# The queries of two heads issued in pairs on TensorE, in slots three, five, six and seven of each group

## What is computed

```python
x = x + tanh(g_xattn) * xattn(ctx_1024, layernorm(x))   # 8 heads of 128
x = x + tanh(g_ffn) * moe(layernorm(x))                 # 8 experts, the best 2 of each row
# xattn(media, latents), per batch element:
q = ln(latents) @ Wq + bq
k, v = split(concat(ln(media), ln(latents)) @ Wkv + bkv)
out = softmax(q @ k.T / sqrt(128)) @ v @ Wo + bo
```

## Time and profile before

| | |
|---|---|
| median of 3 runs | 797.5 us |
| lowest and highest run | 796.06 and 798.2 us |
| the profiled execution, span from first to last instruction | 795.7 us |
| TensorE busy | 760.7 us, 96% of the span, 5392 matmuls |
| TensorE weight loads | 643.6 us, 81% |
| VectorE busy | 528.3 us, 66% |
| ScalarE busy | 496.9 us, 62% |
| GpSimd busy | 446.1 us, 56% |
| mean granted TensorE clock | 0.993 of full speed |

### The profile page before, as it was taken

How to read it: one execution, slowest core, us unless ns; L and a number is a source line. 1 busy time by engine, 2 the same in 40 slices (tenths; PEclk the granted TensorE clock), 3 DMA queues, 4 the chain that set the end, 5 groups by cost and what they waited for, 6 DMA issues and landing times.

```text
span 795.7 us, 17460 instructions
## 1 busy us (share of the span) xinstructions
PE 760.7 (96%) x5392; PEld 643.6 (81%) x5392; DVE 528.3 (66%) x1829; ACT 496.9 (62%) x1630; POOL 446.1 (56%) x455
## 2 busy tenths in 40 slices
PE   7999999999999999999999999999999999979788
PEld 6778777777888988778988878898877888868765
DVE  5636677685857567677658776776868567565536
ACT  3677777676766566766656667565567665554522
POOL 2233264646552544785655586665568566556664
PEclk9999999999999999999999999999999999999999
DMA  7735151542454642174754226664414555634523
GB/s 198 209 150 194 60 213 69 211 146 81 145 188 154 205 153 72 38 231 143 237 189 143 65 76 218 206 212 163 127 54 140 180 191 188 212 112 116 154 77 87
DMA packets 119791, 119.42 MB, mean 150 GB/s; under 512 B 14585, under 2 KB 94994, under 8 KB 119698
## 3 DMA queue, kind: packets, MB, share of 16 engines
q1 hardware_dynamic: 111088, 102.41, 39.1%
q0 software_dynamic: 7680, 15.74, 6.8%
q10 hardware_dynamic: 930, 0.15, 0.1%
HBM read 35.94 MB, written 41.55 MB: 97 GB/s over the span
## 4 chain that ended last, share of the span: by engine, by line
PE 77%; issue 6%; POOL 6%; DVE 5%; ACT 4%; DMA 1%; another core or an unknown queue 1%; SPq 1%; POOLq 0%; ACTq 0%; DVEq 0%
PE shared L1426 13%; PE batch L1364 11%; PE batch L1377 11%; PE hid_ps L1294 8%; PE xy_ps L1308 7%; PE batch L1372 6%; PE shared L1217 3%; PE shared L1219 3%; PE shared L1218 3%; ACT probs L746 3%; PE batch L1308 2%; POOL probs L676 2%; PE xy_ps L1271 2%; POOL yg L666 2%; PE batch L1354 2%
## 5 line engine op out<-in xcount | busy, mean ns | idle before, releaser
L676 POOL TENSOR_TENSOR probs<-probs,rsums 128x512 f32<-128x512 f32 x128 | 132.9, 1039 | 231.7 <-DVE rsums L1147 230.1
L746 ACT ACTIVATE probs<-batch,neg_max 128x128 f32<-128x128 f32 x512 | 180.5, 374 | 2.0 <-DVE neg_max L1151 2.0
L651 POOL DMA_INDIRECT sorted_x<-xn,row_of x120 | 124.4, 1036 | 33.6 <-issue 28.7
L827 ACT ACTIVATE qT<-shared,tb 128x512 f32<-128x512 f32 x128 | 87.2, 696 | 85.6 <-PE shared L1219 72.4
L1377 PE MATMUL batch<-pT_sb,kvn 128*128 128x512 f32 x256 | 133.7, 604 | 2.9 <-ACT pT_sb L754 2.9
L1364 PE MATMUL batch<-kvT,qT 128*128 128x128 f32 x1024 | 135.4, 275 | 0.8 <-ACT qT L827 0.8
L1426 PE MATMUL shared<-M,oT 128*128 128x128 f32 x1024 | 125.5, 276 | 0.3
L1364 PEld LDWEIGHTS batch<-kvT,qT 128*128 128x128 f32 x1024 | 124.4, 192 | 1.2 <-ACT qT L827 1.2
L1426 PEld LDWEIGHTS shared<-M,oT 128*128 128x128 f32 x1024 | 119.4, 192 | 1.6 <-issue 1.6
L746 ACT ACTIVATION_READ_ACCUMULATOR probs<-batch,neg_max 128x1 f32 x512 | 110.2, 215 | 0.0
L1147 DVE RECIPROCAL rsums<-sums 128x4 f32<-128x4 f32 x128 | 22.7, 178 | 130.4 <-ACT probs L746 119.9
(11 more groups left out here) (168 smaller groups left out, 1243.4 us busy)
## 6 DMA issues: line engine op xcount, KB each, us to landing
wt<-wall SPq DMA_DIRECT2D x124, 321.0 KB
sorted_x<-yg SPq DMA_DIRECT2D x36, 512.0 KB, 4.8
xt<-sorted_x SPq DMA_DIRECT2D x162, 64.0 KB
sorted_y<-y_sb SPq DMA_DIRECT2D x78, 128.0 KB
kv<-in_ctx_dram SPq DMA_DIRECT2D x16, 256.0 KB
kv<-in_x_dram SPq DMA_DIRECT2D x16, 256.0 KB
xres<-in_x_dram SPq DMA_DIRECT2D x32, 128.0 KB
out_dram<-x SPq DMA_DIRECT2D x15, 256.0 KB
```

The costliest lines, as they stand in the source:

```text
L651: nc.gpsimd.indirect_dma_start(xs[k % SETS][:, :], bass.IndirectOffsetOnAxis(ap=row_of[:, g, choice, c:c + 1], axis=0), xn[:, g % 2, c, :] ...
L676: nc.gpsimd.tensor_tensor(pv, pv, rsums[:, m % 2, :].unsqueeze(2).broadcast_to([P, 4, P]), ALU.mult).then_inc(probs_ready, 1)
L746: last = nc.scalar.activation(probs[:, m % 2, c * P:(c + 1) * P], batch_ps[m % BANKS][:, c * P:(c + 1) * P], ACT.Exp, bias=neg_max[:, m % ...
L827: nc.scalar.activation(qT[:, g % 2, :, number, :], sh[:, :].rearrange("p (b i) -> p b i", b=GB), ACT.Identity, bias=tb[:, number:number + ...
```

## The change

The change is in the table `SHARED` alone. In s = 3 and s = 7 both queries stand in place "b", where one stood in "a" and one in "b". In s = 4 there is no query. In s = 5 and s = 6 there are two queries each, both in place "c": heads 2 and 3, then 4 and 5.

```diff
-    3: [("query", 1, 0, "a"), ("query", 1, 1, "b")],
-    4: [("project", 0, 0, "a"), ("turn_x", -1, 0, "b"), ("query", 1, 2, "c")],
-    5: [("router", -1, 0, "a"), ("query", 1, 3, "b"), ("query", 1, 4, "c")],
-    6: [("project", 0, 1, "a"), ("query", 1, 5, "b")],
-    7: [("query", 1, 6, "a"), ("query", 1, 7, "b")],
+    3: [("query", 1, 0, "b"), ("query", 1, 1, "b")],
+    4: [("project", 0, 0, "a"), ("turn_x", -1, 0, "b")],
+    5: [("router", -1, 0, "a"), ("query", 1, 2, "c"), ("query", 1, 3, "c")],
+    6: [("project", 0, 1, "a"), ("query", 1, 4, "c"), ("query", 1, 5, "c")],
+    7: [("query", 1, 6, "b"), ("query", 1, 7, "b")],
```

## The result

| | before | after |
|---|---|---|
| median of 20 runs each, side by side | 796.86 us | 798.34 us |
| lowest and highest | 795.85 and 798.45 | 797.26 and 801.72 |
| span of the profiled execution | 795.7 us | 797.3 us |
| mean granted TensorE clock | 0.993 | 0.992 |

The ratio is 1.002, with a 95% interval of 1.0013 to 1.0028: slower by 0.2%.

The account below looks back on a forecast made before the run. TensorE was taken as the bound, busy 96% of the span, with slack only where no tiles run. There +0.9 us, +0.4 at the start and nothing with tiles took the 797.5 median to 798.8 us, range 795.5 to 802.5.

Parts of the forecast that it names:

- Light stretches: Eight stretches with queries where no sorted tile runs beside attention; slots 5 to 7 mostly sum to 14.89 us, +0.9 together.
- the old wait for the logits goes: Slot 6 without tiles: the query needing the logits' bank comes at +1.68 us after the product, past the old wait's +1.28.
- The price of the pair's hold: Slots 6 and 7 without tiles: ScalarE reads both queries before keeping the product, making them 5.74 and 5.57 us.
- The upper bound: The first read-out also waits for the second query: 0.59 us more in 16 slots, 9.4 us in all.
- Slots with tiles: Seven stretches with sorted tiles beside attention: slot 5 loses 1.41 us, slot 7 gains it, net nothing.
- cover of 0.45 us: Slot 7 with tiles: TensorE needs 6.99 us, the next product is ready at 6.54, so TensorE's work hides ScalarE's delay.
- the tile slots are held too: Slower rival: with tiles, slot 6's pair delays ScalarE beyond what TensorE's work hides, 3.9 us more, 802.7; chance 0.20.
- The idle in slot 7: Without tiles, TensorE idles 0.5 to 0.7 us ahead of the product (L1377), released by ScalarE's copy to pT_sb.
- The start: Before the first batch, the third query stands behind the last fold; the eighth comes at about 27.2, not 26.80: +0.4 us.
- TensorE alone sets the slots: Faster rival: slots 6 and 7 without tiles take 5.47 and 5.00 us, 6.4 less in all, 792.4; chance 0.12.
- A quicker query: Rival: a query takes less than 0.70 us on TensorE, giving 793.8 us; chance 0.01.
- No change: Rival: waits in slots without tiles belong to another chain and trade one for one, 797.5 us; chance 0.06.

Follow-up runs that it names:

- the last experiment: All queries but one ahead of a product, ScalarE keeping the product first, old table before the first batch; 787.16 us, ratio 0.9876 to the kernel before.
- the first experiment: The changed kernel with the old table for queries before the first batch alone; 784.14 us, ratio 1.0023 to the kernel before on that chip.
- the fourth experiment: The changed kernel with all queries but query 2 moved ahead of a product; 775.03 us, ratio 0.9913 to the kernel before on that chip.

## Why the prediction held, point by point

The forecast was 798.8 us with no measurable change the likeliest, and 798.34 came.

- **Light stretches, slots 5 to 7.** Predicted 3.58, 5.74 and 5.57; measured 3.60, 5.73 and 5.59. The sum of 14.89 came as 14.90 to 14.92 from slots 3, 27, 35 and 59, and in the stretch from slot 11, where 16.43 was worked out, 16.40.
- **Sum over the light stretches.** Predicted +0.9. Over slots 4 to 7 the eight give +0.73, +0.26, +0.28, +0.30, -0.72, +0.03, +0.14 and +0.13, in all +1.15. The last two are mis-sized by 0.1 each: the step "the old wait for the logits goes" does not hold there. The second query of slot 6 needs the logits' bank, and VectorE reads that bank late (L983, at 459.28). The query's record starts at 459.55 and is 0.07 longer than without a wait, and slot 6 takes 5.81, elsewhere 5.72 to 5.74. Other slots between 2 and 129 gave back 0.41, of which 0.20 is slot 114 (5.58 became 5.38), which the prediction did not name; in two more executions with the same order there it took 5.44 and 5.25. So the attention stretch as a whole grew by 0.74. That this lies as near to +0.9 as it does is in part luck: the light stretches cost 0.25 more than predicted, and the others, put at nothing, gave 0.41 back.
- **The price of the pair's hold.** It was the unsure term, with bounds 6.4 below and 9.4 above. The value between them was right. Taking the hold away gives 5.8 to 5.9 back; what is missing to the 6.4 is about eight times the 0.07 by which slot 7 stays above 5.00. The upper bound, a first read-out that waits for the second query, did not come: ScalarE reads the first at 158.95, 1.86 after the product, and both in one row of 1.37. The wait that a third query brings is of another kind, a query that waits for a read-out.
- **Slots with tiles.** Predicted nothing, under a cover of 0.45 us: measured slots 5 and 7 6.44 and 5.58 before, 5.04 and 6.97 after, and from the product of slot 43 to that of slot 47 it is 24.91 in both. Slot 7 was worked out as 6.99. The rival "the tile slots are held too" falls for this change, and three queries behind a product show the mechanism behind it at work.
- **The idle in slot 7** was put at 0.5 to 0.7 and is 0.43, ended by the copy to pT_sb as said. The slot's length was right; the row counts idle from the modelled end of the query's last matmul, 0.17 after the point where a next one would have started.
- **The start.** Predicted +0.4, measured +0.47 from first query to first scores. The fold came 0.31 earlier against the first query (0.38 worked out), and the pairs run at 0.85 a query. The rows after the change, TensorE from the last fold to the first scores, answer to the earlier trace rows:

```profile
23.00 0.46 PE L1250 MATMUL batch<-probs 128*128 128x128 f32 x2 [0.36 <-ACT probs L725]
...
23.67 0.48 PE L1217 MATMUL shared<-latT_hi,A_hi 128*128 128x512 f32 x1
...
27.93 0.39 PE L1217 MATMUL shared<-latT_hi,A_hi 128*128 128x512 f32 x1
...
29.57 0.60 PE L1364 MATMUL batch<-kvT,qT 128*128 128x128 f32 x3 [0.78 <-ACT qT L827]
```

  The rest of the 1.02 at the start, 0.55, lies ahead of the first query, which stood at 20.14 in this execution and at 19.59 in that of before. In the eleven profiles it comes between 17.96 and 20.22, and nothing in the change touches it. A part of that spread is the clock: in the five profiles where the first query comes at 19.59 or later, the granted clock between 10 and 20 us is 0.83 in the mean, and in the six where it comes at 18.44 or earlier, it is 1.00. Before and after the change are both of the five, so the 0.55 between them has another cause, which stays open.
- **TensorE alone sets the slots** (792.4) fell: slots 29 to 31 have 14.02 busy of 14.92. **A quicker query** (793.8) fell too: the pair ahead of the product still takes 0.70 a query. **No change** is hard to tell from the forecast by time, but the slots' lengths tell them apart: 4.87 became 3.60 and 3.59 became 5.59.

## What to carry to other kernels

Where two engines hand work round a loop, and one of them serves its queue in a fixed order, an operation that the loop's item has to pass costs the loop its whole wait, even if both engines have time left over. Put extra work ahead of the handoff or into slots whose own work is longer than the loop (here 3.6 us), or let the reader take the loop's item first; here these two gave 0.9% and 0.5%, and 1.1% together, each against the kernel before (the second of them on top of the change's table), where grouping alike operations gave nothing. Before doing it, count the buffers: with two banks, two uses in a row are free and the third waits for the first.

## What the runs showed of the hardware

**The clock can fall at the start.** Busy by stretch of the last experiment, columns as above:

```profile
27.00:30.00 3.00, 3.00 (x24) 3.00 (x24) 2.15 (x8) 1.16 (x7) 0.00 (x0) 0.85 0.54 158
30.00:33.00 3.00, 3.00 (x15) 3.00 (x15) 2.14 (x9) 0.35 (x3) 1.04 (x1) 0.50 0.17 50
33.00:36.00 3.00, 3.00 (x17) 3.00 (x16) 0.36 (x2) 2.69 (x11) 0.73 (x1) 0.51 1.04 324
```

The granted clock is at half, 1.2 GHz, from 30 to 36 us, while TensorE has work all the time, and the first scores to the product of slot 2 take 9.52 us in place of 7.33. Ahead of that TensorE had idled 0.78 before the first scores and then run sixteen matmuls of one column (at 27.92), as it does in every kernel here. The changed kernel passed the same place at full clock:

```profile
27.00:30.00 3.00, 2.14 (x10) 1.41 (x10) 1.68 (x7) 2.13 (x4) 1.25 (x1) 1.00 0.77 167
30.00:33.00 3.00, 3.00 (x29) 3.00 (x28) 2.24 (x8) 1.50 (x8) 0.00 (x0) 1.00 0.10 29
```

A fall at this place is in two of the eleven profiles (the first experiment and the last), both with the old start under a new table, and these are the two whose first scores come earliest (26.99 and 26.92; the next are at 27.41). The kernel before has the same start, its first scores at 28.55 and 7.33 us there, so the table alone does not cause it. What does stays open; it was not tried apart. Nor is it the only fall: five other profiles have the 0.83 between 10 and 20 us named above. In the changed kernel TensorE had there waited 2.03 us for the weights of `Wo`, up to 12.50, and the same two matmuls (L1250) that take 0.39 at 12.88 take 0.64 at 14.12.

**A chip can differ by 2%, all of it in one stage.** The kernel before takes 781.8 us on one chip and 796.6 to 797.5 on the others. It was not profiled on the quick chip, but the first experiment has the changed kernel's order behind the start and shows the same attention stretch there, 659.56. The difference lies behind the product of slot 129: 85.9 to 87.2 us on the quick chip, 100.9 to 101.5 on the others, whatever the kernel. Busy by stretch from 43.7 us behind that product on, first the change on an ordinary chip, then the fourth experiment on the quick one, which is further on in its work by then:

```profile
740.00:760.00 20.00, 14.56 (x112) 14.00 (x111) 9.98 (x27) 10.97 (x21) 12.02 (x14) 0.91 0.53 146
```

```profile
730.00:750.00 20.00, 20.00 (x136) 16.18 (x135) 10.78 (x31) 8.73 (x16) 15.14 (x16) 1.00 0.48 129
```

On the ordinary chip TensorE idles 5.4 of 20 us in the last tiles, ahead of hidden and output layers, for nothing that the profile names. The granted clock is 0.91 in that row; all seven profiles on ordinary chips have such falls between 700 and 760 us, and none of the four on the quick chip. The cause of the idle was not tried, and whether a kernel could avoid it is not known. It is the reason why ratios here are taken on one chip.
